# A TensorE-bound hybrid block on one core: MLP and second attention merged into one loop over pairs of images

## What is computed

```
x = x + proj(window_attention(layernorm1(x)))   # 14x14 windows, 12 heads of 16, relative positions
x = x + lin2(gelu(lin1(layernorm2(x))))         # MLP 192 -> 768 -> 192, exact gelu
t = t + W_out(causal_attention(ln(t)))          # second attention: 256 tokens, 3 heads of 64
t = t + soft_moe(ln(t))                         # 4 experts, 256 slots each, softmax dispatch/combine
```

## Time and profile before

| what | us |
|---|---|
| runs | 1032.81, 1033.30, 1023.52 |
| median of the runs | 1032.81 |
| the profiled execution, own time | 1029.97 |
| its span in the trace | 1028.3 |
| around the span (own time less span) | 1.7 |
| PE / PEld / DVE / ACT / POOL busy | 912.1 / 724.0 / 474.6 / 462.3 / 181.5 |
| mean granted TensorE clock | 0.931 |

### The profile page before, as it was taken

How to read it: one execution, slowest core, us unless ns; L and a number is a source line. 1 busy time by engine, 2 the same in 40 slices (tenths; PEclk the granted TensorE clock), 3 DMA queues, 4 the chain that set the end, 5 groups by cost and what they waited for, 6 DMA issues and landing times.

```text
span 1028.3 us, 14917 instructions
## 1 busy us (share of the span) xinstructions
PE 912.1 (89%) x5408; PEld 724.0 (70%) x5408; DVE 474.6 (46%) x1025; ACT 462.3 (45%) x927; POOL 181.5 (18%) x257
## 2 busy tenths in 40 slices
PE   2878878878887879999889988999899989998998
PEld 1755765575575558876767765998598958995898
DVE  4767586684756663342444364105520452036101
ACT  5766457456645734333243343243433334244423
POOL 3040031004000002114122025001500051004200
PEclk9899879987998989995796999999999999999999
DMA  6010000001000000001010020000000000000000
GB/s 179 1 35 2 1 14 20 0 0 31 0 1 0 1 25 20 11 11 32 0 31 10 1 108 1 1 1 16 0 0 0 15 0 0 0 15 1 1 1 16
DMA packets 12708, 15.44 MB, mean 15 GB/s; under 512 B 5313, under 2 KB 10561, under 8 KB 12545
## 3 DMA queue, kind: packets, MB, share of 16 engines
q1 hardware_dynamic: 10656, 9.46, 3.0%
q0 software_dynamic: 2016, 5.51, 1.9%
HBM read 13.39 MB, written 1.57 MB: 15 GB/s over the span
## 4 chain that ended last, share of the span: by engine, by line
PE 67%; DVE 15%; ACT 8%; issue 8%; DMA 1%; SPq 0%; POOL 0%; DVEq 0%; ACTq 0%; POOLq 0%
PE ps L217 19%; PE ps L1343 12%; PE ps L1083 6%; PE ps L1271 6%; ACT area L839 5%; PE ps L1358 4%; DVE area L269 4%; PE ps L1164 3%; PE ps L1213 2%; PE ps L966 2%; PE ps L1006 2%; PE ps L1123 1%; PE ps L1211 1%; DVE dstat L702 1%; PE ps L1124 1%
## 5 line engine op out<-in xcount | busy, mean ns | idle before, releaser
L217 PE MATMUL ps<-xs,ws 128*128 128x512 f32 x460 | 132.3, 437 | 12.3 <-DVE xs L496 7.9
L1343 PE MATMUL ps<-area 128*128 128x192 f32 x768 | 127.4, 326 | 0.0
L1343 PEld LDWEIGHTS ps<-area 128*128 128x128 f32 x768 | 124.8, 190 | 2.0 <-issue 0.5
L217 PE MATMUL ps<-ws,wx 128*128 128x512 f32 x480 | 116.3, 398 | 1.2 <-DVE ws L723 1.2
L217 PEld LDWEIGHTS ps<-xs,ws 128*128 128x128 f32 x460 | 92.6, 209 | 34.3 <-issue 9.5
L217 PEld LDWEIGHTS ps<-ws,wx 128*128 128x128 f32 x480 | 89.2, 188 | 22.8 <-DVE ws L723 2.9
L934 ACT ACTIVATE area<-ps,bcol 128x512 f32<-128x512 f32 x96 | 65.8, 689 | 86.7 <-PE ps L217 86.6
L1083 PE MATMUL ps<-ident,area 112*98 112x112 f32 (+1 forms) x480 | 68.2, 285 | 37.4 <-ACT area L839 37.4
L734 DVE TENSOR_TENSOR area<-ps,area 128x384 f32<-128x384 f32 x32 | 17.9, 559 | 177.8 <-PE ps L1343 177.8
L839 ACT ACTIVATE area<-ps,nm 112x196 f32<-112x196 f32 (+1 forms) x240 | 85.5, 439 | 26.3 <-DVE nm L604 25.9
L1083 PEld LDWEIGHTS ps<-ident,area 112*98 112x98 f32 (+1 forms) x480 | 50.6, 139 | 63.6 <-ACT area L839 63.2
(11 more groups left out here) (161 smaller groups left out, 1466.3 us busy)
## 6 DMA issues: line engine op xcount, KB each, us to landing
stage<-in_wall POOLq DMA_DIRECT2D x42, 128.0 KB, 2.4
area<-in_w2e SPq DMA_DIRECT2D x1, 2304.0 KB, 8.5
out<-xres SPq DMA_DIRECT2D x4, 384.0 KB, 2.6
xres<-in_x SPq DMA_DIRECT2D x1, 1152.0 KB, 7.5
area<-in_wall SPq DMA_DIRECT2D x2, 512.0 KB, 5.9
area<-in_w2a SPq DMA_DIRECT2D x1, 576.0 KB, 3.8
room<-in_rel SPq DMA_DIRECT2D x4, 128.0 KB, 5.2
xres<-in_x SPq DMA_DIRECT2D x1, 384.0 KB, 3.2
```

Of the source, the lines that this page charges most:

```text
L217: last = mm(out_, l, r, start=n == 0, stop=n == len(pairs) - 1)
L1343: last = mm(ps[:, 4 + b, s * D:s * D + D], hTd[:, m, b * T + s * P:b * T + s * P + P], w2x[:, e * MC + m, :], start=m == 0, stop=m == MC - 1)
```

## The change

`body_b` and `body_c` of every engine go, and `body_bc` takes their place. The MLP of pair 0 is written out ahead of the loop. Pass n of the loop runs the second attention of pair n and, in its first three passes, the MLP of pair n+1 (`first_layer`, `second_layer`), in an order of PE passes written out by hand. Each pass has two fronts: `early`, the norm of the MLP of pair n+1 (in the last pass that of pair 0 for the experts), and `late`, the norm of the second attention of pair n+1. Both go through the one `xs`, so within a pass `xs` holds first the attention's input and then the MLP's.

Other things change with it. The MLP's first layer has two banks (5 and 6) in place of four. Scores have two banks in place of three, and turned weights one in place of two. The row sums come from ACT (`accum_out` of the exponentials), DVE takes their reciprocal (`shares`), and POOL multiplies the weights by it (`scaled`) before PE turns them; the column of ones, the division, and the turning back of `co` go. PE's product with the values (`values`) now has the values as weights and writes the result already turned, with DVE copying it out (`turned_out`). The projection goes by image (`project_image`). The functions computed are the same.

The diff, cut to its core, with indentation reduced by twelve (lines removed are those of the functions printed above):

```diff
 nm = sb("nm", [P, 2, HG])
 rs = sb("rs", [P, 2, HG])
 cnm = nm.rearrange("p a b -> p (a b)").rearrange("p (a b) -> p a b", b=2)
+crs = rs.rearrange("p a b -> p (a b)").rearrange("p (a b) -> p a b", b=2)
+crc = sb("crc", [P, 4, 2])
 AREA = 16640
...
+(hT, w2l, cqk, cq2, cv, cp, cpt) = views([
+(MC, N), (MC, D), (2, N), (2, N), (NT, D), (4, 3 * P), (2, 3 * P)])
...
 c_qk, c_v, c_qt, c_ve, c_s, c_nm, c_p, c_t, c_pt, c_o = (
 sem(n) for n in ("c_qk", "c_v", "c_qt", "c_ve", "c_s", "c_nm", "c_p", "c_t", "c_pt", "c_o"))
...
+c_rc, c_pn, c_on = (
+sem(n) for n in ("c_rc", "c_pn", "c_on"))
 d_l, d_ra, d_rv, d_rt, d_pm, d_nm, d_bt, d_bc, d_cs, d_ce = (
...
     for s in range(ST):
         nc.gpsimd.tensor_tensor(ct[:, s, :], ct[:, s, :], bc, ALU.add).then_inc(d_cs, 1)
...
+def expert_chunks(count):
+    nonlocal k1, chunk
+    for _ in range(min(count, NCHUNK - chunk)):
+        split_chunk(chunk, k1, experts=True, final=chunk == NCHUNK - 1)
+        k1 += 4
+        chunk += 1
+def next_norm(f):
+    nonlocal k1
+    k1 += 1
+    norm_scale(f, NT, k1)
+def scaled(u):
+    pool.wait_ge(c_rc, u + 1)
+    to = cp[:, u % (2 * AH) % 4]
+    rc = crc[:, u % (2 * AH) % 4]
+    nc.gpsimd.tensor_scalar(to[:, 0:P], to[:, 0:P], rc[:, 0:1], None, ALU.mult)
+    nc.gpsimd.tensor_scalar(to[:, P:3 * P], to[:, P:3 * P], rc[:, 1:2], None, ALU.mult).then_inc(c_pn, 1)
+next_norm(PAIRS)
+pool.wait_ge(o_res, 1 + 2 * PAIRS)
+expert_chunks(2)
+next_norm(PAIRS + 1)
+for it in range(PAIRS):
+    next_norm(PAIRS + 2 + 2 * it)
+    for u in range(4):
+        scaled(it * 2 * AH + u)
+    expert_chunks(2)
+    if it < PAIRS - 1:
+        next_norm(PAIRS + 3 + 2 * it)
+    for u in range(4, 2 * AH):
+        scaled(it * 2 * AH + u)
+    expert_chunks(1)
+expert_chunks(NCHUNK)
+for n in range(1, PAIRS):
+    dispatch_combine(n - 1)
+    next_norm(3 * PAIRS + n)
 dispatch_combine(PAIRS - 1)
...
 loop(dve, body_a)
...
+residual(0, (5, 6), b_y, 0, b_res)
+dve.wait_ge(b_res, 1 + 2)
+front_norm(PAIRS + 1, 0, NT)
+front_split(PAIRS + 1, NT, (b_h, MC))
+def body_bc(it, nxt):
     n = 2 * AH
     base = it * n
...
+    early = it * 2 + (PAIRS + 2), it + 1 if nxt else 0, NT
+    late = it * 2 + (PAIRS + 3), it + 1, NT
+    def maxima(u):
+        dve.wait_ge(c_s, base + u + 1)
+        if u >= 4:
+            dve.wait_ge(c_p, base + u - 3)
+        V.reduce_max(cnm[:, u % 4, 0:1], ps[:, u % 2, 0:P], AX.X, negate=True)
+        V.reduce_max(cnm[:, u % 4, 1:2], ps[:, u % 2, P:3 * P], AX.X, negate=True).then_inc(c_nm, 1)
+    def shares(u):
+        dve.wait_ge(c_p, base + u + 1)
+        if u >= 4:
+            dve.wait_ge(c_pn, base + u - 3)
+        V.reciprocal(crc[:, u % 4, :], crs[:, u % 4, :]).then_inc(c_rc, 1)
+    def turned_out(b):
+        dve.wait_ge(c_o, it * 2 + b + 1)
+        V.tensor_copy(ot0[:, b * T:b * T + T], ps[:, 3 + b, 0:T])
+        V.tensor_copy(ot1[0:R1, b * T:b * T + T], ps[0:R1, 3 + b, T:2 * T]).then_inc(c_on, 1)
+    front_stats(*early)
+    front_scale(*early, range(NT))
+    for b in range(2):
+        dve.wait_ge(c_v, it * 2 + b + 1)
+        V.tensor_tensor(cv[:, 2 * b:2 * b + 2, :], ps[:, 3 + b, 0:2 * D].rearrange("p (t d) -> p t d", d=D),
+                        brow[:, 1, :].unsqueeze(1).broadcast_to([P, 2, D]), ALU.add).then_inc(c_ve, 1)
+    maxima(0)
+    maxima(1)
+    front_split(early[0], NT, (c_v, 2 * it + 2))
+    shares(0)
+    shares(1)
+    maxima(2)
+    shares(2)
+    maxima(3)
+    shares(3)
+    if nxt:
+        residual_image(it + 1, (5, 6), b_y, it + 1, b_res, 0)
+    maxima(4)
+    if nxt:
+        residual_image(it + 1, (5, 6), b_y, it + 1, b_res, 1)
+        dve.wait_ge(b_res, 2 * it + 5)
+        gated(dve, 1)
+        front_stats(*late)
+    maxima(5)
+    shares(4)
+    shares(5)
+    if nxt:
+        front_scale(*late, range(NT))
+    turned_out(0)
+    turned_out(1)
+    if nxt:
+        front_split(late[0], NT, (b_h, MC * it + 2 * MC))
+    residual(it, (3, 4), o_proj, it + PAIRS, o_res)
+loop(dve, body_bc)
 def body_d(it, nxt):
...
 act.wait_ge(o_res, 1 + 2 * PAIRS)
...
+def first_layer(n, m):
+    if m == 0:
+        act.wait_ge(b_y, 1 + n * 2)
+    act.wait_ge(b_h, n * MC + m + 1)
+    A.activation(hT[:, m, :], ps[:, 5 + m % 2, :], ACT.Gelu, bias=bcol[:, L1B + m:L1B + m + 1])\
+        .then_inc(b_gelu, 1)
+for m in range(MC):
+    first_layer(0, m)
+front_turned(PAIRS + 1, NT, 0)
+def body_bc(it, nxt):
+    n = 2 * AH
+    base = it * n
+    early, late = it * 2 + (PAIRS + 2), it * 2 + (PAIRS + 3)
+    affine = N2 if nxt else 0
+    def exponentials(u):
+        act.wait_ge(c_nm, base + u + 1)
+        if u >= 4:
+            act.wait_ge(c_t, base + u - 3)
+        A.activation(cp[:, u % 4, 0:P], ps[:, u % 2, 0:P], ACT.Exp, bias=cnm[:, u % 4, 0:1],
+                     accum_out=crs[:, u % 4, 0:1])
+        A.activation(cp[:, u % 4, P:3 * P], ps[:, u % 2, P:3 * P], ACT.Exp, bias=cnm[:, u % 4, 1:2],
+                     accum_out=crs[:, u % 4, 1:2]).then_inc(c_p, 1)
+    def turned(u):
+        act.wait_ge(c_t, base + u + 1)
+        A.activation(cpt[:, u % 2, :], ps[:, 2, 0:3 * P], ACT.Copy).then_inc(c_pt, 1)
     act.wait_ge(c_qk, it * 3 + 1)
     A.activation(cqk[:, 0, :], ps[:, 0, :], ACT.Identity, scale=AD ** -0.5, bias=bcol[:, CQB:CQB + 1])
     A.activation(cq2[0:AD, 0, :], ps[0:AD, 2, :], ACT.Identity, scale=AD ** -0.5, bias=bcol[0:AD, CQB + 1:CQB + 2])
     A.activation(cq2[0:AD, 1, :], ps[AD:P, 2, :], ACT.Identity, bias=bcol[AD:P, CKB + 1:CKB + 2])\
         .then_inc(c_qt, 1)
...
+    front_turned_part(early, affine, 0)
+    exponentials(0)
+    front_turned_part(early, affine, 1)
+    exponentials(1)
+    if nxt:
+        first_layer(it + 1, 0)
+        first_layer(it + 1, 1)
+    turned(0)
+    exponentials(2)
+    exponentials(3)
+    turned(1)
+    if nxt:
+        for m in range(2, MC):
+            first_layer(it + 1, m)
+    turned(2)
+    exponentials(4)
+    turned(3)
+    exponentials(5)
+    turned(4)
+    turned(5)
+    if nxt:
+        front_turned_part(late, 0, 0)
+        front_turned_part(late, 0, 1)
+loop(act, body_bc)
 def body_d(it, nxt):
     for s in range(ST + 4):
         if s < ST and s % 2 == 0:
...
 pe.wait_ge(w_split, A_CHUNKS - QKV_CHUNKS)
 pe.wait_ge(o_res, 1 + 2 * PAIRS)
...
+def first_layer(n, m):
+    if m < 2:
+        pe.wait_ge(b_res, 1 + n * 2)
+    else:
+        pe.wait_ge(b_gelu, n * MC + m)
+    product(ps[:, 5 + m % 2, :], (CL1 + m * P, CL1 + m * P + P), xcols(0, N)).then_inc(b_h, 1)
+def second_layer(n, b):
+    if b == 0:
+        pe.wait_ge(ld_l2, 16)
+        pe.wait_ge(b_gelu, n * MC + MC)
+    for j in (2 * b, 2 * b + 1):
+        dst = ps[:, 5 + b, (j % 2) * D:(j % 2) * D + D]
         mm(dst, ot1[L2ROW:L2ROW + 1, 0:P], wproj[L2ROW:L2ROW + 1, 0, 1, :], start=True, stop=False)
         for m in range(MC):
             if j == 0 and m == MC - 1:
...
+                pe.wait_ge(b_gelu, n * MC + MC + 1)
             last = mm(dst, hT[:, m, j * P:j * P + P], w2l[:, m, :], start=False, stop=m == MC - 1)
...
+    last.then_inc(b_y, 1)
+pe.wait_ge(ln_split, PAIRS + 1)
+for m in range(MC):
+    first_layer(0, m)
+for b in range(2):
+    second_layer(0, b)
+front_turn(PAIRS + 1, NT)
+def body_bc(it, nxt):
+    n = 2 * AH
+    base = it * n
+    early, late = it * 2 + (PAIRS + 2), it * 2 + (PAIRS + 3)
+    def scores(u):
+        b, h = u // AH, u % AH
+        if u >= 2:
+            pe.wait_ge(c_p, base + u - 1)
+        if h < 2:
+            rows = slice(AD * h, AD * h + AD)
+            q, k = cqk[rows, 0, :], cqk[rows, 1, :]
+        else:
+            q, k = cq2[0:AD, 0, :], cq2[0:AD, 1, :]
+        t0 = b * T
+        bank = ps[:, u % 2, :]
+        mm(bank[:, 0:P], q[:, t0:t0 + P], k[:, t0:t0 + P], start=True, stop=False)
+        mm(bank[:, 0:P], identb[:], maskb[:], start=False, stop=True)
+        mm(bank[:, P:3 * P], q[:, t0 + P:t0 + T], k[:, t0:t0 + T], start=True, stop=False)
+        mm(bank[:, 2 * P:3 * P], identb[:], maskb[:], start=False, stop=True).then_inc(c_s, 1)
+    def turn(u):
+        pe.wait_ge(c_pn, base + u + 1)
+        if u:
+            pe.wait_ge(c_pt, base + u)
+        for k in range(3):
+            last = tr(ps[:, 2, k * P:k * P + P], cp[:, u % 4, k * P:k * P + P], ident[:])
+        last.then_inc(c_t, 1)
+    def values(u):
+        b, h = u // AH, u % AH
+        pe.wait_ge(c_pt, base + u + 1)
+        rows, c0 = (slice(AD * h, AD * h + AD), 0) if h < 2 else (slice(0, AD), T)
+        dst = ps[rows, 3 + b, c0:c0 + T]
+        of = slice(AD * h, AD * h + AD)
+        mm(dst, cv[:, 2 * b, of], cpt[:, u % 2, 0:T], start=True, stop=False)
+        last = mm(dst[:, P:T], cv[:, 2 * b + 1, of], cpt[:, u % 2, T:3 * P], start=False, stop=True)
+        if h == AH - 1:
+            last.then_inc(c_o, 1)
+    def project_image(b):
+        pe.wait_ge(c_on, it * 2 + b + 1)
+        for j in (2 * b, 2 * b + 1):
+            dst = ps[:, 3 + b, (j % 2) * D:(j % 2) * D + D]
```

(54 more changed lines are left out.)

180 lines of the change are left out of this document (8 added, 172 removed).

## The result

| | before | after |
|---|---|---|
| median of the runs, us | 1033.05 (1023.52 to 1039.76, 4 runs) | 1061.16 (1056.71 to 1064.37, 4 runs) |
| ratio of times, 95% interval | | 1.0405 [1.0356, 1.0454] |
| profiled execution, own time / span | 1029.97 / 1028.3 | 1064.37 / 1062.7 |
| mean granted clock | 0.931 | 0.923 |
| first MLP product to first expert product | 219.57 | 252.20 |

The account below looks back on a forecast made before the run. PE was taken to set both stages, with waits and half clock besides. Full-clock schedule 599.3 against 601.5, clock spells +15.1 and fast/fp32 changes +1.5 gave +14.4 on 1029.97: 1044 us, range 1024 to 1061.

Parts of the forecast that it names:

- The split behind turn, scores, turn and scores: DVE's split of the early front in a merged pass: ends at 13.3 us, PE idle 2.9 before the first MLP product.
- Product 4: MLP first-layer product in a merged pass, waiting for ACT's gelu: starts at 24.8 us, 1.65 us idle.
- The late split: End of a merged pass: ACT's copy and DVE's split behind the late front's last turn leave PE idle 1.75 us.
- The table load on the path: ACT's table switches between gelu and exponential delay turn 2 and product 4 by 1.0 and 1.65 us a merged pass.
- The bare transition: After the first MLP, ahead of the loop: nothing covers pair 0's front, 11.8 us, once.
- The clock: Slow spells: 7.6 us on queries and keys, 4.5 on the last pass, 1 in each merged pass, sum 15.1.
- the scaling: POOL's multiplication of a unit's weights ahead of its turn: 0.8 us for two operations, ends 0.5 and 1.6.
- old waits of some 5 us: PE's waits in the old MLP and attention passes of a pair, replaced by the merged pass's own 11 us.
- A: Rival: the clock holds through the merged stretch, above 0.95, giving 1029 to 1031 us; chance 0.26.
- B: Rival: PE fills, idle falls to 2 us a pass, merged pass under 46 us, time 1017; chance 0.13.
- C: Rival: POOL's scaling takes 1.6 us or more a unit, some 3 us a pass, time 1056; chance 0.14.
- D: Rival: table switches beside waiting matmuls cost the load once more, 7.7 us in three passes, time 1052; chance 0.05.

Follow-up runs that it names:

- e6: Changed kernel with needless filler passes in every long wait of PE from the first MLP on, last pass included; 1039.77 us, ratio to before 1.0154.
- k1: Kernel before, with fillers in its second attention: 6 ahead of the next queries and keys, 4 each ahead of last turn and projection; 1023.60 us, ratio 0.9938.
- k3: k2 with 6 more fillers ahead of the wait for ACT's copies of queries and keys and 5 ahead of the first turn; 1001.50 us, ratio 0.9857.
- e12: e6 with Identity in place of the MLP's gelu, so no table loads in the loop, and without the 5 fillers ahead of product 4; 1038.32 us.
- e3: Changed kernel with eleven fillers ahead of PE's wait for the early front's split, nothing else; 1059.04 us, ratio to before 1.0438.
- k2: k1 with 7 and 8 fillers also in two waits of the window attention; 1010.94 us, ratio to before 0.9949.
- e8: e6 without the reciprocals and POOL's scaling of the weights, and with fewer fillers ahead of turns; 1041.92 us, ratio to before 1.0182.
- e7: e6 with the scaling of the weights moved from POOL to DVE; 1051.98 us, ratio to before 1.0293.

## Why the prediction was right and where it failed

**Waits and places: right.** The split behind turn, scores, turn and scores: first product 13.3 forecast, 13.2 measured, idle 2.9 and 2.89. Product 4 at 24.8: 28.2 in the changed kernel, and 24.7 as soon as the wait ahead was filled. The late split 1.75: 1.69. New values product 0.65: from its start to the next operation 0.65 once in a pass and 0.80 elsewhere (e6). The table load on the path 2.65: 2.0. The bare transition 11.8: 11.9, from the end of the first MLP at 404.00 to the start of pass 0 at 415.94.

**The clock: the term that failed most.** I charged 15.1 us, of which 7.6 on the queries and keys, 4.5 on the last pass and 1 in each merged pass, "dense blocks end a slow spell soon". The queries and keys ran at full clock in two passes (3.74) and took 5.99 and 5.31 in the others, so they lost 3.8 us, half of the charge. The merged passes lost 7.0, 4.4 and 5.3 us with them and the last at least 5.2: 22.1 in place of 15.1 with the 0.2 of the transition. Less the queries and keys it is 12.9 us inside the three merged passes, 4.3 each. The step that failed is the 1 us a pass: a spell behind the 2.9 us wait lasted 9.5 us although three dense products stood in it, since the products in it took 2.5 us in place of 1.4.

**The passes at full clock: 11 us too short.** 51.5, 52.5, 52.5 and 30.6 were 54.1, 54.9, 55.0 and 34.2, the last with up to 1.8 us of surplus fillers; without them it is some 9 us. Turn 4, forecast at 44.35, came at 46.0 in e6. DVE and POOL ahead of turn 4 in that pass (start 521.60), from its timeline:

```profile
564.57 0.15 DVE L681 RECIPROCAL crc<-rs 128x2 f32<-128x2 f32 x1
564.64 1.04 POOL L328 TENSOR_TENSOR rstd<-rstd,mhalf 128x4 f32<-128x4 f32 x1
565.68 0.65 POOL L434 TENSOR_SCALAR area<-area,crc 128x128 f32<-128x128 f32 x1
566.32 1.23 POOL L435 TENSOR_SCALAR area<-area,crc 128x256 f32<-128x256 f32 x1
```

The order is the forecast one, the reciprocal behind maxima 5, POOL at the late front's root. POOL ends the root at 44.1 (forecast 43.5), and the scaling is 1.88 us in place of 0.8: 0.6 and 1.1 of the 1.65. Turn 5 then waits 0.29 for POOL and the remainder of the pass is 0.5 longer than summed. I had put ends of 0.5 and 1.6 around my value for the operation; it was at the upper end alone, and above it beside DVE's front. The Trainium skill, "GPSIMD Engine Reference", section "Elementwise — side-by-side cycle accounting", has a best case of 769 ns for 512 elements; an estimate from it for 128 and 256 elements is 0.6 us a unit. The rows have 1.57, so the measurement decides.

**What the merge is measured against.** I wrote that the old pair of passes took 19.0 + 31.0 us at full clock, with "old waits of some 5 us" to be won. The 31.0 were not at full clock: the 10.7 in them hold the slow queries and keys, 5.30 in place of 3.75. k1 has 19.0 + 29.4, fillers included. So a merged pass never had 50 us to beat, but 48.4. And the slow spells of the old attention, which made it look improvable, went by fillers and without any reordering (k1 in the profiled execution, k3 in all six runs by their granted clock).

**In sum**, for the profiled execution: forecast +14.4, measured +34.4. The missing 20.0 are 7.0 of clock, 11.1 in the passes as e6 has them (of which up to 1.8, the surplus fillers, belong to the clock), 1.7 up to pass 0 (32.1 us in place of 30.2, of which 0.2 is counted with the clock; nearly all of it lies in the first MLP, which took 20.2 us in place of 18.4, and not in the gap behind it), 1.9 by which the window attention ended later in this execution, less the 1.5 for changes between fast and fp32 passes, a term that no run shows: in the new order of e6 a token tile took 2.67 us (2.66 in the earlier trace rows), queries and keys 3.7 and the scores of a unit 1.24 to 1.37 (1.27 in the earlier trace rows). The terms are rounded.

**The rivals.** A (the clock holds) fell; with fillers it holds, but for 1039.8, not 1029. B (PE fills) fell: with the computation whole no merged pass was under 54 us, and B needed 46. Its ground was also read wrongly: DVE and ACT are each busy for under half of the stretch, but 167 of 224.5 us together. C named the right engine: 1.5 to 1.9 us a unit, but it cost some 1.5 us a pass where C had 3. That the measured 1061 is so near to C's 1056, and to the end of the range that I drew from C and one long spell, is luck: most of the excess is clock and steps of the schedule that C does not name. D fell by e12.

## What to carry to other kernels

Before two loops are merged to fill the matrix engine's waits, run each of them with cheap filler passes in those waits: a profile whose clock column is at 1.00 shows what the loops cost at full clock, and that may be the larger part of what the merge is meant to win (here 25 us, 219.6 against 194.6). Count the price of the edits that the merge forces (fewer banks, a detour over another engine, an uncovered first transition) against that figure, not against the slow one. Where a chain of dependent steps makes a wait, a filler does not end it but can keep the work behind it fast. One filler is not enough, since the slow spell can move to the next wait that has none (e3, k2), and fillers longer than the wait cost their own time (k3, the last pass of e6).

## What the runs showed of the hardware that I had not expected

The clock fell behind waits of PE no longer than 1.47 us (k2, pass 0 at 0.63) and 1.39 us (e3), and once in thin unit work with no wait above 0.78 us (k2, last pass). Yet e8 held 1.00 through waits of 1.53 us, where e7, with 1.51 in the same place, did not: the length of one wait does not decide it, and what does is open. A spell could last for nearly a whole pass (25 us at 0.57 in the last one after). POOL's instruction on 128x256 elements took 0.92 us, and 1.23 when DVE scaled a front beside it. And most of the spread of this kernel goes with the clock: the kernel before took 1011.2 us at a mean granted clock of 0.955 and 1037.3 at 0.923 on one chip, while k3, at 0.980 to 0.995 in all its runs, stayed within 8.1 us.
